# Ordering the last feed-forward, the shared expert and the expert copies of a four-stage sequence kernel

## The chip, the cores and the metric

The kernel runs on one core of a Trainium2 chip. The metric is the device time of one execution in microseconds. Each engine (PE is TensorE, DVE is VectorE, ACT is ScalarE, POOL is GpSimd, SP is SyncE, which issues most of the DMAs) works off its own instructions in a fixed order and waits for the others on semaphores. All orders are written out by hand.

## The reference

The input x has 4 sequences of 512 tokens, 128 wide. Four stages run one after the other, each added to x behind a layer norm:

```
x = x + recurrence(layernorm(x))        # h = h*A + x_t along the tokens, then h @ BC
x = x + local_layers(layernorm(x))      # 2 layers: local attention (8 heads, window 64), then
                                        #   h = norm(shift(y)); y = y + (a * gelu(g)) @ w2 + b2
x = x + attention(layernorm(x))         # 8 heads of 16 over the 512 tokens of a sequence
x = x + moe(layernorm(x))               # shared = (silu(x @ sg) * (x @ su)) @ sd
                                        # routed: expert argmax(x @ gate) of 32, rows scaled by
                                        #   sigmoid(max), silu(x @ g_e) * (x @ u_e) @ d_e
```

## The kernel before, in words

**Blocks.** The local layers run as 8 blocks of one sequence and one layer, each with 4 tiles of 128 tokens. Block 7 is the last sequence in the last layer. The generator `layer_steps()` yields the order of all steps, and every engine walks through the same list and issues its own part of each step. The steps of a block's feed-forward are `y_att` (DVE adds the product of the attention into y, L1062, and copies the unshifted half, L1066), `shift` (PE moves the other half by one token with two matmuls, L1534 and L1535, into bank 2 of PSUM; ACT copies it out, L783), `ff_stats`, `ff_rstd`, `ff_apply` (DVE L953, L957, L964, POOL L602), `hnT` (PE transposes, ACT scales, L1542 and L791), three times `up` (PE L1551, ACT gelu L797, DVE product L1072), `down` (PE L1560 in 24 matmuls, DVE L1081) and `base` (POOL).

**Drain and front.** After the loop over the 32 tiles, a tail of `layer_steps()` drains blocks 6 and 7. Steps of the global attention (`l1`) are woven into it: for sequence 1 the front is `apply` (DVE L964 into `y`), `pre` (PE transposes into bank 2, L1650, ACT L822), `qk` (PE L1656 and L1657, ACT) and `split` (ACT, POOL, and then the SP's stores). For sequence 0 there are six `max` steps (PE L1671 makes scores, DVE L1244 reduces them in 1.2 us each), and `sums`, two DVE reductions. `max` uses banks 4 and 5, `up` 20 and `qk` 1 banks 6 and 7. The following list, `l1_steps()`, starts with 16 more `max` steps, the last six of which need the query and key stacks of sequence 1. Work on the probabilities follows.

**Shared expert and slots.** The tail of `l1_steps()` holds the last sequence's norm and routing, and the shared expert of the four sequences. Its steps: `s_up b i` (PE, four matmuls, L1590), `silu` (ACT L803), `gate` (DVE product L1197), `s_down b` (PE, 16 matmuls, L1627, after both gates of b and after the `add` of b-2), `add b` (DVE adds to x, L1202; the semaphore `x4s` counts these). The steps `s_up`, `rank` and `row` take three pairs of banks in turn. For the routing: `route` (PE, then `choose` on DVE), `rank` (PE counts; 15 small DVE steps of `slots_b`, ending in L1182, give the slot of each row), `scale` (DVE multiplies the rows by their score, L1125), `scatter` (POOL, four indirect DMAs for each sequence, L691), `experts` and `row` (the list of experts, DVE L1297). The SP waits for all scatters, then loads the first rows (L571) and the row numbers (L573) and stores the four sequences of x as their `add` is done (L578).

**Routed experts.** 24 tiles of 4 x 32 rows, four experts each, run in a pipeline. Experts 1 to 3 of a tile have their weights copied from the resident `wx` to `w_copy`: two by DVE (`weights_one`, L1211), one by ACT (`weights_two`, L811). The expert's number is read from memory into a register (`value_load`, L1205 on DVE) before each copy. `copies 0` and `copies 1` are steps of the tail; the copies of tile 2 stand after it, behind a wait for the fourth `add`, since their places overlap the shared expert's products `act_s` in `region_b`. Then `gated(0)` and `gated(1)` (DVE L1358) follow, and the loop. POOL adds each tile's result to the output with an indirect DMA (L718), once the four stores have landed.

The change touches `places`, `l1_steps`, `layer_steps`, the ACT and the DVE code ahead of the routed loop.

Of the kernel before, what the change touches and what calls it, by code (L numbers as in the profile page):

```python
# [15 lines left out]
BATCH, SEQ = 4, 512  # L16
# [32 lines left out]
PER = 4  # L49
# [3 lines left out]
EW = 2 * INTER + IC * P  # L53
# [17 lines left out]
def build(nc, A, out):  # L71
    with ExitStack() as ctx:
# [10 lines left out]
        region_b = sb("region_b", [P, 10400])  # L83
# [147 lines left out]
        def copies(*places):  # L231
            return [region[:, at:at + EW] for region, at in places]

        places = copies(*((region_r, 2048 + n * EW) for n in range(PER)), (region_b, 0), (region_b, EW),
                        *((region_b, 4112 + n * EW) for n in range(2 * PER)), (region_r, 0))
        w_copy = [places[n * 3:n * 3 + 3] for n in range(WBUF)]
        xs_dram = nc.dram_tensor("xs_dram", (SLOT_ROWS, ROW), FP).ap()

# [33 lines left out]
        def l1_steps():  # L272

            n = BATCH * 16  # L280
            early = {7: (("val", 1),), 8: (("stat", 2),), 10: (("apply", 2),), 14: (("pre", 2),), 16: (("qk", 2),),
                     17: (("val", 2),), 18: (("split", 2),), 20: (("load", 2),)}
            late = {1: (("stat", 3),), 3: (("apply", 3),), 6: (("pre", 3),), 8: (("qk", 3),), 9: (("split", 3),), 13: (("load", 3),), 17: (("val", 3),),
                    43: (("rstat", 0), ("rstat", 1)), 44: (("rapply", 0),), 45: (("rapply", 1),), 47: (("rpre", 0),), 48: (("rpre", 1),),
                    50: (("rstat", 2),), 51: (("route", 0),), 52: (("rapply", 2),), 53: (("route", 1), ("scale", 0)),
                    55: (("rpre", 2), ("scale", 1)), 57: (("route", 2),), 59: (("scale", 2),), 60: (("rank", 0),),
                    61: (("scatter", 0),)}
            for m in range(DRAIN_MAX, LEAD):
                yield "max", m // 16, m % 16
                if m == 16:  # L290
                    yield "shift", 0, 0
                for what, b in early.get(m, ()):
                    yield what, b, 0
            for g in range(n):
                yield "probs", g // 16, g % 16
                m = g + LEAD
                if m < n:
                    yield "max", m // 16, m % 16
                if m % 16 == 0 and 16 < m <= n:
                    yield "shift", m // 16 - 1, 0  # L300
                if g % 16 == 1 and g > 16:
                    yield "end", g // 16 - 1, 0
                for what, b in late.get(g, ()):
                    yield what, b, 0

            last = BATCH - 1
            yield from (("s_up", 0, 0), ("end", last, 0), ("silu", 0, 0), ("rstat", last, 0), ("scatter", 1, 0), ("scatter", 2, 0),
                        ("gate", 0, 0), ("s_up", 0, 1), ("silu", 0, 1), ("gate", 0, 1), ("s_up", 1, 0), ("silu", 1, 0),
                        ("rapply", last, 0), ("s_up", 1, 1), ("gate", 1, 0), ("rpre", last, 0), ("silu", 1, 1), ("s_down", 0, 0),
                        ("gate", 1, 1), ("route", last, 0), ("add", 0, 0), ("s_up", 2, 0), ("silu", 2, 0), ("rank", 1, 0),  # L310
                        ("s_down", 1, 0), ("scale", last, 0), ("scatter", last, 0), ("gate", 2, 0), ("s_up", 2, 1), ("silu", 2, 1),
                        ("add", 1, 0), ("experts", 0, 0), ("gate", 2, 1), ("s_up", 3, 0), ("silu", 3, 0), ("s_down", 2, 0),
                        ("row", 0, 0), ("gate", 3, 0), ("s_up", 3, 1), ("silu", 3, 1), ("copies", 0, 0), ("gate", 3, 1),
                        ("add", 2, 0), ("copies", 1, 0), ("s_down", 3, 0), ("add", 3, 0))

        def up_banks(n):

# [9 lines left out]
        def layer_steps():  # L327
# [12 lines left out]
            def l1(*items, b=0, i=0):  # L340
                return [("l1", (what, b, i)) for what in items if what]
# [4 lines left out]
            for i in range(NTILES):  # L346
                t, k = i % NT, i // NT - 1
                up = {3: HC * k, 0: HC * (k - 1) + 1, 1: HC * (k - 1) + 2, 2: -1}[t]
                yield from of(NTILES, ("probs", i))
                yield from of(BLOCKS * HC, ("to_gelu", up))  # L350
                yield from of(NTILES, ("v", i + 3), ("ssq", i + 3))
                yield from early.get(i, ())
                if t == 0:
                    yield from of(BLOCKS, ("y_att", k))
                yield from l1({27: "stat", 28: "apply"}.get(i))
                if i == NTILES - 1:
                    yield from l1("stat", b=1)
                if t == 1:
                    yield from of(BLOCKS, ("ff_stats", k))
                yield from of(NTILES, ("vals", i), ("heads", i + 1), ("masks", i + 1))  # L360
                if t == 0:
                    yield from of(BLOCKS, ("shift", k))
                if t == 2:
                    yield from of(BLOCKS, ("hnT", k))
                if t == 3:
                    yield from of(BLOCKS, ("stream", k + 3))
                yield from fronts.get(i, ())
                yield from l1(*{28: ("pre",), 29: ("split", "load"), 30: ("wv",)}.get(i, ()))
                yield from of(NTILES, ("rotsum", i + 2))
                if t == 1:  # L370
                    yield from of(BLOCKS, ("ff_rstd", k))
                yield from of(NTILES, ("norm", i + 3))
                yield from of(BLOCKS * HC, ("up", up))
                if t == 2:
                    yield from of(BLOCKS, ("down", k - 1))
                if t == 3:
                    yield from of(BLOCKS, ("base", k))
                yield from of(NTILES, ("scores", i + 1))
                if i < NTILES - 1:
                    yield from of(BLOCKS * HC, ("to_exp", up))  # L380
                yield from of(NTILES, ("oT", i), ("qk", i + 4))
                if i == NTILES - 1:
                    yield "up", HC * k + 1
                    yield from l1("max")
                yield "wo", i
                if t == 1:
                    yield from of(BLOCKS, ("ff_apply", k))
                if i == 28:
                    yield from l1("qk")
                yield from of(NTILES, ("rot", i + 3))  # L390
            b, m = BLOCKS - 1, HC * BLOCKS
            yield from l1("zero")
            yield from l1("zero", b=1)
            yield from l1("apply", b=1)
            yield "y_att", b
            yield from l1("pre", b=1)
            yield "shift", b
            yield from l1("max", i=1)
            yield from (("ff_stats", b), ("ff_rstd", b), ("up", m - 4))
            yield from l1("qk", b=1)  # L400
            yield "ff_apply", b
            yield from l1("sums")
            yield "hnT", b
            yield from l1("split", b=1)
            yield "down", b - 1
            yield from l1("max", i=2)
# [318 lines left out]
        def _(a):  # L725
# [79 lines left out]
            def expert_two(j):  # L805
                return a.value_load(exp_of[0:1, PER * j + 3:PER * j + 4], min_val=0, max_val=EXP - 1)

            def weights_two(j, e):

                need(a, M["y_mm"], j - WBUF + 1)  # L810
                act_(w_copy[j % WBUF][2], wx[:, bass.ds(e, 1), :].rearrange("p a n -> p (a n)"), ACT.Copy)\  # L811
                    .then_inc(M["w_two"], 1)
# [105 lines left out]
            def back_sb(j):  # L918
                a.wait_ge(M["actT_mm"], j + 1)
                need(a, M["y_mm"], j - 1)  # L920
                act_(actT[j % 2], bank(4 + j % 2)[:, 0:INTER], ACT.Copy).then_inc(M["actT_sb"], 1)

            tokens_sb(0)
            tokens_sb(1)
            a.wait_ge(M["x4s"], BATCH)
            weights_two(2, expert_two(2))
            gate_sb(0)
            tokens_sb(2)
            e = expert_two(3)
            gate_sb(1)  # L930
            back_sb(0)
            for j in range(PAIRS):
                if j + 3 < PAIRS:
                    weights_two(j + 3, e)
                if j + 4 < PAIRS:
                    e = expert_two(j + 4)
                if j + 2 < PAIRS:
                    gate_sb(j + 2)
                if j + 3 < PAIRS:
                    tokens_sb(j + 3)  # L940
                if j + 1 < PAIRS:
                    back_sb(j + 1)
# [3 lines left out]
        def _(v):  # L946
# [419 lines left out]
                    v.wait_ge(ys_out[j % AHEAD], 16 * (j // AHEAD))  # L1366
                d.tensor_copy(ys[j % AHEAD], bank(6 + j % 2)[:, 0:P]).then_inc(M["y_sb"], 1)  # L1367

            weights_one(2, [expert_of(2, w) for w in (1, 2)])
            pair = [expert_of(3, w) for w in (1, 2)]  # L1370
            gated(0)
            gated(1)
# [555 lines left out]
```

## Time and profile before

| | |
|---|---|
| median of 3 runs | 682.47 us (680.77 to 684.91) |
| the profiled execution | 679.96 us, of it span of the instructions 678.1 us |
| busy | PE 87%, DVE 76%, ACT 53%, POOL 45% of the span |
| mean granted clock of TensorE | 0.958 |

An engine's busy share is a mean over very different stages. The start of the first feed-forward of block 7 lies at about 424 us, the last six `max` ahead of the probabilities at about 470 us, the shared expert from 586 us to 620 us, the routed loop from there to the end. A timeline row gives the start, the duration, the engine and line, what is written and read, and in brackets how long the engine was idle before it and what released it. A chain row gives start, duration, engine, output and line of one piece of the chain that ended last.

### The profile page before, as it was taken

The numbers are of one execution on the slowest core, as the hardware profiler recorded it, in microseconds if no ns is written. First come the engines' busy times: TensorE is split into PE (matmuls) and PEld (weight loads), VectorE is DVE, ScalarE is ACT, GpSimd is POOL, SyncE is SP. The second block draws the span as 40 slices with busy tenths as digits, with TensorE's granted clock in tenths as the row PEclk, the third lists the DMA queues.
The fourth block names the chain that finished last, engine by engine and source line by source line (L and its number), as shares of the span: only waits on it lengthen the run. The fifth ranks groups of instructions, "written<-read, shape, count | busy, mean of one in ns | idle before, by whom it ended". The sixth has DMA issues, their size and how long they took to land.

```text
span 678.1 us, 14399 instructions
## 1 busy us (share of the span) xinstructions
PE 587.9 (87%) x5382; PEld 343.5 (51%) x5382; DVE 517.0 (76%) x935; ACT 360.5 (53%) x566; POOL 306.5 (45%) x247
## 2 busy tenths in 40 slices
PE   3767678899999999999999888778899989987994
PEld 2244455666766767667667556432223324454442
DVE  6777888988889788888888754578877786574883
ACT  0223224477567575675774664312575667734872
POOL 2676444656354546464755633313120001251786
PEclk9768989999999999999999999896899999998998
DMA  8303000101010101010101035060966226214451
GB/s 262 85 17 117 17 17 17 26 17 25 18 33 9 34 17 26 18 25 17 34 9 34 17 82 122 19 127 4 217 202 189 95 94 212 71 32 106 60 66 11
DMA packets 33298, 44.03 MB, mean 65 GB/s; under 512 B 9249, under 2 KB 24653, under 8 KB 32461
## 3 DMA queue, kind: packets, MB, share of 16 engines
q1 hardware_dynamic: 29260, 40.99, 22.8%
q0 software_dynamic: 3968, 2.12, 2.4%
q8 instruction: 44, 0.72, 0.4%
q14 instruction: 26, 0.21, 0.1%
HBM read 27.54 MB, written 8.41 MB: 53 GB/s over the span
## 4 chain that ended last, share of the span: by engine, by line
PE 47%; DVE 29%; issue 11%; ACT 6%; POOL 4%; DVEq 1%; DMA 0%; POOLq 0%; ACTq 0%
PE ps L1551 5%; PE ps L1582 4%; DVE ssum L1012 4%; DVE smx L1042 3%; PE ps L1560 3%; PE ps L1687 3%; DVE mneg L1244 3%; PE ps L1773 3%; ACT region_r L853 2%; PE ps L1671 2%; DVE region_b L1020 2%; DVE region_r L1029 2%; DVE region_r L1037 2%; PE ps L1794 2%; PE ps L1504 2%
## 5 line engine op out<-in xcount | busy, mean ns | idle before, releaser
L624 POOL TENSOR_TENSOR rnorm<-ssum_c,neg_half 128x16 f32<-128x16 f32 x32 | 94.3, 2947 | 108.2 <-DVE ssum_c L1015 106.7
L636 POOL TENSOR_TENSOR region_r<-region_b,region_w 128x512 f32<-128x512 f32 x64 | 82.8, 1315 | 38.7 <-DVE region_b L1020 38.1
L1244 DVE TENSOR_REDUCE mneg<-ps 128x2 f32<-128x1024 f32 x64 | 77.1, 1219 | 22.2 <-PE ps L1671 21.2
L853 ACT ACTIVATE region_r<-ps 128x1024 f32<-128x1024 f32 x64 | 63.2, 1024 | 34.0 <-PE ps L1687 33.9
L746 ACT ACTIVATE region_w<-ps 128x1024 f32<-128x1024 f32 x32 | 32.8, 1025 | 64.2 <-PE ps L1438 64.2
L1437 PE MATMUL ps<-region_w,hT 128*128 128x512 f32 x64 | 37.6, 672 | 20.5 <-DVE region_b L1020 19.6
L600 POOL TENSOR_TENSOR var_eps<-mv,eps 128x4 f32<-128x4 f32 x20 | 8.0, 400 | 103.5 <-DVE mv L957 103.5
L731 ACT ACT_TABLE_LOAD x39 | 50.0, 1283 | 1.4 <-PEq L1920 0.7
L718 POOL DMA_INDIRECT out<-region_r x24 | 38.2, 1592 | 22.4 <-DVE region_r L1367 14.7
L1020 DVE TENSOR_TENSOR region_b<-ps,rnorm 128x1024 f32<-128x1024 f32 x32 | 39.1, 1221 | 11.8 <-POOL rnorm L624 10.9
L1551 PE MATMUL ps<-region_w 128*114 128x512 f32 x96 | 46.7, 610 | 0.6 <-ACT region_w L763 0.6
L1504 PEld LDWEIGHTS ps<-region_b,pts 128*64 128x64 f32 x512 | 32.2, 137 | 24.8 <-issue 24.8
L772 ACT ACTIVATE pts<-ps 128x512 f32<-128x512 f32 x64 | 34.9, 595 | 16.6 <-PE ps L1489 16.5
L1523 PEld LDWEIGHTS ps<-region_w,oT 128*128 128x128 f32 x256 | 34.0, 194 | 18.2 <-issue 11.4
L1012 DVE TENSOR_REDUCE ssum<-region_w 128x16 f32<-128x1024 f32 x32 | 38.7, 1211 | 4.9 <-ACT region_w L746 4.9
L1037 DVE TENSOR_TENSOR region_r<-region_r 128x1024 f32<-128x1024 f32 x32 | 41.4, 1294 | 0.3
L1042 DVE TENSOR_REDUCE smx<-ps 128x8 f32<-128x1024 f32 x32 | 38.9, 1215 | 2.3 <-PE ps L1479 2.3
L1045 DVE TENSOR_TENSOR region_b<-ps,smx 128x1024 f32<-128x1024 f32 x32 | 39.2, 1224 | 1.1
L1029 DVE TENSOR_TENSOR region_r<-region_b,region_w 128x1024 f32<-128x1024 f32 x32 | 39.7, 1240 | 0.0
L1504 PE MATMUL ps<-region_b,pts 128*64 128x65 f32 x512 | 36.6, 225 | 2.2 <-ACT pts L772 2.2
L778 ACT ACTIVATE oT<-ps 128x512 f32<-128x512 f32 x32 | 18.8, 586 | 35.2 <-PE ps L1512 35.2
L1523 PE MATMUL ps<-region_w,oT 128*128 128x128 f32 x256 | 34.4, 278 | 3.0 <-ACT oT L778 3.0
(277 smaller groups left out, 1419.0 us busy)
## 6 DMA issues: line engine op xcount, KB each, us to landing
region_w<-in_wx SPq DMA_DIRECT2D x16, 768.0 KB, 4.5
region_b<-region_w SPq DMA_DIRECT2D x56, 130.0 KB, 2.3
parts_dram<-region_b SPq DMA_DIRECT2D x6, 384.0 KB, 2.6
xs_dram<-region_w SPq DMA_DIRECT2D x1, 1548.0 KB, 7.3
region_w<-in_wqkv SPq DMA_DIRECT2D x2, 768.0 KB, 8.8
pts<-xs_dram SPq DMA_DIRECT2D x24, 64.0 KB, 2.0
region_w<-parts_dram SPq DMA_DIRECT2D x3, 384.0 KB, 6.8
region_b<-parts_dram SPq DMA_DIRECT2D x3, 384.0 KB, 7.3
```

What stands on the lines that cost most here:

```text
L624: g.tensor_tensor(rnorm[:, :], ssum_c[n % 2][:, :], neg_half[:, :], ALU.pow).then_inc(S["rnormed"], 1)
L636: g.tensor_tensor(dst, src, tab, ALU.mult).then_inc(S["rot_bb"], 1)
L853: act_(dst, bank(l1_bank[what, b, i], of=2), ACT.Exp).then_inc(T["ex"], 1)
L1012: d.tensor_reduce(ssum[:, :], sq.rearrange("p (h d) -> p h d", d=DH), AX.X, ALU.add).then_inc(S["ssq"], 1)
L1020: d.tensor_tensor(qn[n % 2].rearrange("p (h d) -> p h d", d=DH), bank(qk_bank(n), of=2).rearrange("p (h d) -> p h d", d=DH), rnorm[:, :].u ...
L1029: d.tensor_tensor(rot[n % 2].rearrange("p (z h d) -> p z h d", z=2, h=HEADS), qn[n % 2].rearrange("p (z h d) -> p z h d", z=2, h=HEADS), t ...
L1037: d.tensor_tensor(rot[n % 2], rot[n % 2], rotb[n % 2], ALU.add).then_inc(S["rotated"], 1)
L1042: d.tensor_reduce(smx[n % 2][:, :], sc, AX.X, ALU.max).then_inc(S["smax"], 1)
L1244: d.tensor_reduce(mneg[b % 2][:, 2 * i:2 * i + 2], bank(l1_bank[what, b, i], of=2) .rearrange("p (q t) -> p q t", q=2), AX.X, ALU.max, neg ...
L1504: last = mm(ps[w * WIN:(w + 1) * WIN, c0:c0 + VW], pts[n % 2][:, j, w * WIN:(w + 1) * WIN], vals[:, t, h, :], start=True, stop=True)
L1523: last = mm(bank(3)[:, t * P:(t + 1) * P], oT[n % 2][:, c, :], wo[k // BATCH][:, c, :], start=(c == 0), stop=(c == 3))
L1551: last = mm(ps[0:HW, n0 * BANK:(n0 + 1) * BANK], w1[k // BATCH][:, g, c, :], hnT, start=True, stop=True)
```

## The change

In the tail of `layer_steps()`, `y_att 7` moves ahead of `max 0` and of the front of sequence 1, `shift`, `ff_stats`, `ff_rstd` and `up 20`, `ff_apply` follow at once, and `apply`, `pre`, `qk` of sequence 1 and `max 1` come between or behind; `sums` moves behind `qk 1`. In the tail of `l1_steps()`, `scale 3` and the last scatter move ahead of or beside `rank 1`, the additions 0 and 1 move behind the slots, `row` ahead of the last `s_up`, `s_down 2` behind that, and a new step `copies 2` stands ahead of `add 3`. So that it can, the places of `w_copy[2]` become free of `act_s` (one of them lies in `rot_b` now), and the wait of ACT for `x4s` moves behind its first steps of the routed pipeline.

```diff
-                        *((region_b, 4112 + n * EW) for n in range(2 * PER)), (region_r, 0))
+                        (region_b, 4112), (rot_b, 0), (region_b, 4112 + 3 * EW),
+                        *((region_b, 4112 + n * EW) for n in (1, 2, 4, 5, 6, 7)))
...
-                        ("gate", 1, 1), ("route", last, 0), ("add", 0, 0), ("s_up", 2, 0), ("silu", 2, 0), ("rank", 1, 0),
-                        ("s_down", 1, 0), ("scale", last, 0), ("scatter", last, 0), ("gate", 2, 0), ("s_up", 2, 1), ("silu", 2, 1),
-                        ("add", 1, 0), ("experts", 0, 0), ("gate", 2, 1), ("s_up", 3, 0), ("silu", 3, 0), ("s_down", 2, 0),
-                        ("row", 0, 0), ("gate", 3, 0), ("s_up", 3, 1), ("silu", 3, 1), ("copies", 0, 0), ("gate", 3, 1),
-                        ("add", 2, 0), ("copies", 1, 0), ("s_down", 3, 0), ("add", 3, 0))
+                        ("gate", 1, 1), ("route", last, 0), ("s_up", 2, 0), ("silu", 2, 0), ("scale", last, 0), ("rank", 1, 0),
+                        ("scatter", last, 0), ("s_down", 1, 0), ("s_up", 2, 1), ("silu", 2, 1), ("gate", 2, 0), ("experts", 0, 0),
+                        ("s_up", 3, 0), ("silu", 3, 0), ("gate", 2, 1), ("add", 0, 0), ("add", 1, 0), ("row", 0, 0),
+                        ("s_up", 3, 1), ("silu", 3, 1), ("gate", 3, 0), ("s_down", 2, 0), ("copies", 0, 0), ("gate", 3, 1),
+                        ("s_down", 3, 0), ("copies", 1, 0), ("add", 2, 0), ("copies", 2, 0), ("add", 3, 0))
...
                 if i == NTILES - 1:
                     yield "up", HC * k + 1
-                    yield from l1("max")
                 yield "wo", i
...
             b, m = BLOCKS - 1, HC * BLOCKS
+            yield "y_att", b
+            yield from l1("max")
             yield from l1("zero")
+            yield "shift", b
             yield from l1("zero", b=1)
+            yield from (("ff_stats", b), ("ff_rstd", b))
             yield from l1("apply", b=1)
-            yield "y_att", b
+            yield from (("up", m - 4), ("ff_apply", b))
+            yield from l1("max", i=1)
             yield from l1("pre", b=1)
-            yield "shift", b
-            yield from l1("max", i=1)
-            yield from (("ff_stats", b), ("ff_rstd", b), ("up", m - 4))
+            yield "hnT", b
             yield from l1("qk", b=1)
-            yield "ff_apply", b
             yield from l1("sums")
-            yield "hnT", b
             yield from l1("split", b=1)
             yield "down", b - 1
...
-            a.wait_ge(M["x4s"], BATCH)
-            weights_two(2, expert_two(2))
             gate_sb(0)
...
             back_sb(0)
+            a.wait_ge(M["x4s"], BATCH)
...
-            weights_one(2, [expert_of(2, w) for w in (1, 2)])
             pair = [expert_of(3, w) for w in (1, 2)]
```

## Rows read from the trace of the kernel before

**Rows 1.** The page: busy times and the granted clock in 40 slices.
```profile
PE 587.9 (87%) x5382; PEld 343.5 (51%) x5382; DVE 517.0 (76%) x935; ACT 360.5 (53%) x566; POOL 306.5 (45%) x247
...
PEclk9768989999999999999999999896899999998998
```

**Rows 2.** Timelines by engine, drain of block 7: DVE, then PE, ACT, POOL.
```profile
422.25 1.22 DVE L1244 TENSOR_REDUCE mneg<-ps 128x2 f32<-128x1024 f32 x1
423.38 1.11 DVE L964 TENSOR_SCALAR y<-xr,mv,rstd 128x128 f32<-128x128 f32 x4
424.40 0.68 DVE L1062 TENSOR_TENSOR region_r<-region_r,ps 128x512 f32<-128x512 f32 x1
...
429.50 0.86 DVE L953 BATCH_NORM_STATS2 stats<-region_b 128x6 f32<-128x128 f32 x4
...
432.48 1.10 DVE L964 TENSOR_SCALAR region_b<-region_b,mv,rstd 128x128 f32<-128x128 f32 x4
...
437.93 0.69 DVE L1081 TENSOR_TENSOR xr<-region_r,ps 128x512 f32<-128x512 f32 x1 [2.09 <-PE ps L1560]
...
426.22 0.67 PE L1534 MATMUL ps<-region_r,down_one 128*128 128x256 f32 x2 [0.96 <-ACT region_r L822]
...
432.82 1.10 PE L1656 MATMUL ps<-region_r,region_w 128*128 128x512 f32 x2 [1.77 <-DVE region_b L1072]
...
435.05 2.84 PE L1560 MATMUL ps<-region_w,region_b 114*128 114x128 f32 x24
...
427.51 0.38 ACT L783 ACTIVATE region_b<-ps 128x256 f32<-128x256 f32 x1 [1.44 <-PE ps L1535]
...
431.14 1.02 POOL L602 TENSOR_TENSOR rstd<-var_eps,neg_half 128x4 f32<-128x4 f32 x1
```

**Rows 3.** The chain that ended last, in the same stretch.
```profile
428.32 2.74 PE ps L1551 x4
...
442.81 1.72 PE ps L1551 x4
```

**Rows 4.** Stretches of 2 us: busy times, granted clock, DMA share, GB/s.
```profile
428.00:430.00 2.00, 2.00 (x4) 0.81 (x4) 1.64 (x4) 0.00 (x0) 0.00 (x0) 0.50 0.00 0
...
460.00:462.00 2.00, 0.88 (x3) 0.13 (x2) 2.00 (x4) 0.00 (x0) 0.00 (x0) 0.50 0.00 0
...
618.00:620.00 2.00, 2.00 (x10) 1.65 (x9) 0.66 (x2) 0.13 (x1) 0.00 (x0) 0.50 0.99 46
```

**Rows 5.** Timelines by engine, from the slots to the last addition: DVE, then PE, SP.
```profile
607.13 0.17 DVE L1182 CAST region_r<-region_r 128x4 uint32<-128x4 f32 x1
...
607.69 0.69 DVE L1125 TENSOR_TENSOR region_b<-region_b,region_r 128x512 f32<-128x512 f32 x1
...
613.14 0.25 DVE L1297 TENSOR_SCALAR region_r<-ps 1x96 int32<-1x96 f32 x1 [2.40 <-PE ps L1644]
...
615.16 1.03 DVE L1211 COPY region_r<-region_w 128x768 f32 x2 [1.19 <-issue]
...
619.66 0.69 DVE L1202 TENSOR_TENSOR xr<-xr,ps 128x512 f32<-128x512 f32 x1 [1.34 <-PE ps L1627]
...
609.03 1.98 PE L1590 MATMUL ps<-region_b,region_r 128*128 128x512 f32 x4 [1.87 <-DVE region_b L1197]
...
616.84 2.78 PE L1627 MATMUL ps<-region_r,region_b 128*128 128x128 f32 x16 [1.83 <-DVE region_b L1197]
...
615.25 1.75 SPq L571 DMA_DIRECT2D pts<-xs_dram  x4
```

**Rows 6.** Timelines: DVE ahead of the routed loop, POOL's first and last output.
```profile
622.68 1.03 DVE L1211 COPY region_b<-region_w 128x768 f32 x2 [2.33 <-issue]
624.36 0.75 DVE L1358 TENSOR_TENSOR region_r<-region_r,ps 128x256 f32<-128x256 f32 x2 [0.65 <-ACT region_r L916]
...
628.62 1.61 POOL L718 DMA_INDIRECT out<-region_r  x1 [14.71 <-DVE region_r L1367]
...
672.95 1.55 POOL L718 DMA_INDIRECT out<-region_r  x1 [0.30 <-issue]
```

## The prediction

> **What bounds the kernel now.** I read the page first. PE is busy 87% of the span and DVE 76% [rows 1], so neither is the bound throughout, and the granted clock has dips below 9 around slices 26 to 29 and near the end. The views that decide are the timelines of the two places that the edits touch, with the chain of waits laid over them.
>
> In the drain of block 7 the chain changes hands from step to step. DVE is free for the last attention product at 422.25, but reduces `max 0` (1.22) and applies the front of sequence 1 (1.11) before `y_att` starts at 424.40. The shift matmuls start at 426.22, 1.1 after the 425.1 at which y was ready: they share bank 2 with `pre 1`, and the bracket names ACT, which reads that. The shifted half is out at 427.9, but the statistics start at 429.50, behind `max 1`. The `up` in the middle of this runs 2.74 [rows 3] with the clock at 0.50 [rows 4], where another takes 1.72 [rows 3]. `ff_apply` starts at 432.48. Then PE does `qk 1` from 432.82, transposes, and starts `down 6` at 435.05, whose sum goes out at 437.93 [rows 2].
>
> At the other end the reader is to see three waits of PE or DVE, each for something that the order put late: PE idles 1.87 until `gate 2 0` (behind the slots and `scale`), 1.83 until the last gate (behind the list of experts and its first copies), and DVE needs 1.19 and 2.33 for register loads [rows 5, 6]. From `gated(0)` at 624.36 on, the loop is a fixed train: the first output leaves POOL at 628.62 and the last at 672.95 [rows 6], 44.33 for 23 steps, 1.93 each.
>
> **The change, drain of block 7.** No arithmetic instruction is added or removed; what counts is when the last links come. New times, from the old durations:
> - `y_att` starts at 422.25 instead of 424.40 (its product is there: PE no longer does `max 0` first). It takes 0.68, the copy about 0.25: y at 422.95.
> - The shift matmuls start at about 423.0, since bank 2 is not yet used by `pre 1`. By the old start and end they take 1.3, ACT 0.38: out at 424.75. DVE fills the time with `max 0`, 423.2 to 424.4, which therefore costs nothing.
> - The statistics run 424.8 to 426.1 (0.86 and the aggregation; from their start at 429.50 to POOL's start at 431.14, less POOL's first small step, it was 1.3). POOL's power takes 1.02 and ends at 427.4. DVE covers this wait with the application for sequence 1 (1.1), to 427.2.
> - PE: `up 20` behind the shift, 424.3 to 426.0 at full clock (1.72), gelu and `gated` (together 1.4, from the old `up`'s end at 431.06 to 432.48); `gated`, half of that, waits for DVE, free at 427.2, and ends at 427.85. `ff_apply` 427.85 to 428.9, against 432.48 before. This is 4.6 earlier.
> - PE: `hnT` 429.0 to 429.6, `qk 1` to 431.35, `down 6` at 431.4 against 435.05: 3.7 earlier. A part of the 4.6 is given back, because `hnT` now stands ahead of `qk 1` and is late for it, while `qk 1` alone could start at 428.6.
> - `sums`, `split`, POOL's parts and the SP's stores follow `qk 1` and come 3 to 3.6 earlier. The `load` behind them is wanted only by `max` steps far back in the following list. `max 1` stands ahead of `sums`, in DVE's slack before `down 6`.
>
> From `down 6` on the order is the old one, so it is carried along: the sum out at 434.2 for 437.93. **Drain: 3.7.** Bounds: 2.15, if only the two DVE steps ahead of `y_att` are saved; 4.6, the advance of `ff_apply`. What follows until the shared expert waits only on things that themselves move (stacks, first weights, statistics), so I let the 3.7 pass undiminished.
>
> **The shared expert.** The time of the slots themselves, 607.30, stays: they wait for PE's ranks. But `scale` (607.2 to 608.38 in the old order) moves into DVE's wait ahead of them, where the addition of sequence 0 and a gap stood, so that:
> - `gate 2 0` is 1.0 earlier, and with it PE's next `s_up`: 608.0 for 609.03. The last scatter of POOL waits for the slots alone and is 1.1 earlier too; the SP's first row loads start at 614.15 for 615.25, land some 2 later, ahead of the use I find below (617).
> - `row` follows that `s_up` at once (609.9) and not `s_down 2` as well: the list of experts at 610.6 instead of 613.14, 2.5 earlier. The two additions stand ahead of it on DVE, in the time that PE needs for the `s_up`.
> - DVE: `gate 3 0` 611.3, loads of two registers (1.19 of visible gap) and `copies 0` (1.03) to 613.5, `gate 3 1` 613.5 to 614.1. PE has done the last `s_up` and `s_down 2` until 613.95, so the gap of 1.83 ahead of `s_down 3` goes: start at 614.15 for 616.84, 2.7 earlier.
> - `s_down 3` took 2.78, with the clock at 0.50 [rows 4]; by the ratio of the two `up`s, 2.74 to 1.72, it would be 1.75 at full clock. It ends at about 616. But DVE now has `copies 1` (1.03), `add 2` (0.69), and `copies 2` (1.03, with 0.3 of loads not hidden) ahead of `add 3`: this one starts at 617.2 and ends at 617.9, for 620.35. **2.4 earlier**, and here the copies take back 1.2 of what PE gives.
> - Behind `add 3` DVE had loads 2.33, copies 1.03, loads 0.65: 4.0 to `gated(0)`. Now only one pair of loads, taken at 2.33: `gated(0)` at 620.2 for 624.36. ACT's side is ready before (rows at 616.5, transposed, matmul, silu by about 619).
>
> **Shared expert and start of the loop: 4.2.** Bounds: 2.4, the advance of `add 3` alone (the moved copies only traded), and 5.3, if the pair of loads costs the 1.19 of the other visible gap. I take the 2.33, since these loads stand behind the same kind of wait. The new places of the copies have the same size, and I give the loop its old step; none of its instructions changes. The stores of the output are the other condition of POOL's start: the DMA engines are filled by the row numbers and the stores (share 0.99, 46 GB/s [rows 4]), all of which start 1.1 to 2.5 earlier, so that they are done at about 623.2, ahead of POOL's 624.4. That is a margin of 1.
>
> **Sum.** 3.7 and 4.2 are 7.9. The profiled execution takes 679.96 with a span of 678.1; it would take 672.1. The median of the three runs is 2.5 above that execution, so 682.47 - 7.9 = 674.6, which is 1.2% less.
>
> **The clock, a rule against it.** The clock stood at 0.50 at 428, 460 and 618 [rows 4], each time after a stretch with little matmul work. By the rows alone, both short dips lose their cause: PE gets `up 20` directly behind the shift, and work without the two gaps of 1.8 at the end.
> The Trainium skill (TensorE: Matmul & The Clock Gate, Part 1) has the activity window of this gate run freely, so that a fall can come at another place in an execution of the same code. By that rule, the new idle spots, small as they are, can be hit: this is the first rival, and the sum would be about 2 less for each hit.
>
> **Rivals.**
> - *The clock falls in the new order.* PE has about 2 of idle time in 426.5 to 429, and again ahead of `gated(0)` (618.5 to 620.7). A fall makes `qk 1` and `down 6` run at half rate, or the first two tiles of the loop, 1.7 to 2.0 each if it lasts as the one at 428 did (about two such 2 us stretches at half speed). One: 676.5. Both: 678.4. For: three dips in the old trace. Against: PE idled longer before these. 0.20.
> - *The drain's gain is absorbed* in the stretch of `max` steps behind it, for instance by a DMA of the stacks that does not move with it. Only 4.2 stay: 678.3. Against: the chain there is DVE's own work. 0.07.
> - *The last steps do not come earlier*: POOL's start is set by the stores and the row numbers, DVE's additions wait for the copies. Then the end gives 0 to 1 and the clock eats part of the drain: about 681. 0.06.
> - *Slower.* The long dip (clock 0.50 at 460 with DVE at 2.00 of 2.00 [rows 4]) costs little because PE waits for DVE's reductions there. If, shifted, it outlasts them and reaches the first probabilities, where PE is the bound, each us of half clock there loses up to 0.5. It decides from some 16 us of dip more, 7.9 lost; at 20 more the time is 684.6. Nothing in the profile speaks for so long a one. 0.05.
>
> **How the numbers follow.** Forecast as worked out 0.62, with an own range of 672 to 677 from the bounds of the two parts (4.6 to 9.9, ends thinned). The range 671.8 to 679.7 takes in the clock rival and the absorbed drain, and leaves out about 0.15. A measurement of this kernel tells a change from none from about 0.5%, or 3.4 us, on: faster is below 679.1. Faster: 0.62, nearly all of 0.20, and half of 0.07, 0.83 in all. Same: the rest of these and the 0.06, 0.12. Slower: 0.05.
>
> **What would show it.** In the trace after: `y_att` of block 7 directly behind the last `gated`, its shift without a wait for ACT, an `up` of 1.7 and not 2.7 behind it, `down 6` at about 431.4. With the drain's 3.7 taken off: L1297 near 606.9, the last `s_up` and `s_down` without gaps, the last L1202 ending near 614.2, the first `gated` near 616.5, the first L718 near 620.7, and 1.93 between outputs. It is wrong if the `max` stretch begins earlier but the probabilities do not, if the loads behind `add 3` cost over 3, or if the loop's step changes.

## The result, and the profile after

The changed kernel takes 676.33 us (median of 8 runs, 672.03 to 679.85); the kernel before, run beside it, took 683.44 (8 runs, 680.77 to 684.91). The ratio is 0.9892, 95% interval 0.9865 to 0.9919. The medians are 7.1 us apart. The forecast was 674.6, faster.

The profiled execution takes 676.56 with a span of 674.8, only 3.4 below the one before (679.96 and 678.1). The page, with the clock in 40 slices:

```profile
PE 587.7 (87%) x5382; PEld 343.2 (51%) x5382; DVE 517.4 (77%) x935; ACT 360.8 (53%) x566; POOL 307.2 (46%) x247
...
PEclk9778999999999999999999999996799999999997
```

The sums are those of [rows 1] within 0.7 us; no work was added. The dip that stood in slice 26 before is gone. Another fall of the clock, from 384.7 to 388.1, is too short to show as a digit in its slice; it lies ahead of everything that was changed. The section on why the prediction was right works out what both did to the 3.4.

First, two rows of the kernel before: the `gated` product from which the drain is counted and the `up` at half clock:

```profile
421.58 0.75 DVE L1072 SCALAR_TENSOR_TENSOR region_b<-ps,b,region_w 114x512 f32<-114x512 f32 x1 [1.41 <-ACT region_w L797]
...
428.12 2.94 PE L1551 MATMUL ps<-region_w 128*114 128x512 f32 x4
```

The drain of block 7, timelines of DVE and then PE in the kernel after, for [rows 2, 3]. The columns are start, duration, engine, line, operation, and in brackets the idle time before it with what ended it.

```profile
423.63 0.75 DVE L1072 SCALAR_TENSOR_TENSOR region_b<-ps,b,region_w 114x512 f32<-114x512 f32 x1 [1.40 <-ACT region_w L798]
424.30 0.68 DVE L1062 TENSOR_TENSOR region_r<-region_r,ps 128x512 f32<-128x512 f32 x1
...
426.56 0.87 DVE L953 BATCH_NORM_STATS2 stats<-region_b 128x6 f32<-128x128 f32 x4
...
429.43 1.11 DVE L964 TENSOR_SCALAR region_b<-region_b,mv,rstd 128x128 f32<-128x128 f32 x4
...
435.68 0.69 DVE L1081 TENSOR_TENSOR xr<-region_r,ps 128x512 f32<-128x512 f32 x1 [1.76 <-PE ps L1559]
...
425.03 0.70 PE L1533 MATMUL ps<-region_r,down_one 128*128 128x256 f32 x2 [0.83 <-DVE region_r L1062]
425.89 1.88 PE L1550 MATMUL ps<-region_w 128*114 128x512 f32 x4
...
432.80 2.84 PE L1559 MATMUL ps<-region_w,region_b 114*128 114x128 f32 x24
```

`y_att` (L1062) begins 0.67 after the start of the last `gated` product, the shift's bracket now names the addition and not ACT, and the `up` behind it runs 1.88 where it ran 2.94 (2.74 as a piece of the chain [rows 3]): it no longer meets a half clock.

The other end, DVE, PE, SP and POOL after, for [rows 5, 6]:

```profile
605.04 0.17 DVE L1182 CAST region_r<-region_r 128x4 uint32<-128x4 f32 x1
608.14 0.25 DVE L1297 TENSOR_SCALAR region_r<-ps 1x96 int32<-1x96 f32 x1
614.64 0.68 DVE L1202 TENSOR_TENSOR xr<-xr,ps 128x512 f32<-128x512 f32 x1
616.65 0.42 DVE L1358 TENSOR_TENSOR region_r<-region_r,ps 128x256 f32<-128x256 f32 x1 [1.32 <-ACT region_r L917]
...
623.21 0.33 PE L1761 MATMUL ps<-ident,pts 128*128 128x128 f32 x1 [2.51 <-DMA pts<-xs_dram]
...
612.46 1.75 SPq L572 DMA_DIRECT2D pts<-xs_dram  x4
614.73 3.65 SPq L579 DMA_DIRECT2D out<-xr  x4
...
623.86 1.83 POOL L719 DMA_INDIRECT out<-region_r  x1 [12.94 <-DMA out<-xr]
628.95 1.69 POOL L719 DMA_INDIRECT out<-region_r  x1 [1.37 <-DVE region_r L1367]
669.64 1.55 POOL L719 DMA_INDIRECT out<-region_r  x1 [0.30 <-issue]
```

And two stretches of 2 us there (busy PE, weight loads, DVE, ACT, POOL; then clock, DMA share, GB/s):

```profile
618.00:620.00 2.00, 2.00 (x31) 0.89 (x27) 1.50 (x4) 2.00 (x6) 0.00 (x0) 1.00 0.97 284
...
624.00:626.00 2.00, 2.00 (x24) 0.69 (x16) 1.15 (x3) 0.92 (x2) 1.70 (x2) 0.50 0.12 33
```

Counted from the start of the span, the first product of the loop (L1358) is 7.7 earlier, but the first output only 4.8, and its bracket names a DMA: the stores of `xr`. PE waits 2.51 for the rows of a later tile, behind them in SP's queue, and then the clock falls.

### The profile page after: what moved, and what is told of

It is laid out like the page before. It is cut to its first block, busy times and chain, and to the rows that moved or that the text cites. A ratio compares the mean times of both kernels' runs of the same rounds, so it can differ in the third digit from the quotient of the medians.

```text
span 674.8 us, 14399 instructions
## 1 busy us (share of the span) xinstructions
PE 587.7 (87%) x5382; PEld 343.2 (51%) x5382; DVE 517.4 (77%) x935; ACT 360.8 (53%) x566; POOL 307.2 (46%) x247
## 4 chain that ended last, share of the span: by engine, by line
PE 47%; DVE 28%; issue 12%; ACT 6%; POOL 4%; DMA 2%; POOLq 0%; DVEq 0%; SPq 0%; ACTq 0%
PE ps L1550 5%; PE ps L1581 4%; DVE ssum L1012 4%; DVE smx L1042 3%; PE ps L1686 3%; PE ps L1559 3%; PE ps L1772 3%; DVE mneg L1244 3%; ACT region_r L854 2%; DVE region_b L1020 2%; PE ps L1670 2%; DVE region_r L1029 2%; DVE region_r L1037 2%; PE ps L1793 2%; DVE region_r L1055 2%
## 5 line engine op out<-in xcount | busy, mean ns | idle before, releaser
L779 ACT ACTIVATE oT<-ps 128x512 f32<-128x512 f32 x32 | 18.8, 586 | 36.2 <-PE ps L1511 36.2
L1478 PEld LDWEIGHTS ps<-region_w 64*64 64x64 f32 x1024 | 28.5, 135 | 17.8 <-issue 15.8
```

## The experiments

The code below shows each edit against the kernel after, with "..." where lines are left out.

All times below that begin with a plus are counted from the start of the same instruction in each trace: in the drain from the last `gated` product (L1072) ahead of `y_att` of block 7 (421.58 before, 423.63 after), at the end from the start of L1182 [rows 5], the slots.

### Each half of the change alone

`drain_only` is the change with only the hunk in `layer_steps()`; the rest is as in the kernel before:

```diff
-                        ("s_down", 3, 0), ("copies", 1, 0), ("add", 2, 0), ("copies", 2, 0), ("add", 3, 0))
...
+                        ("add", 2, 0), ("copies", 1, 0), ("s_down", 3, 0), ("add", 3, 0))
...
+            weights_one(2, [expert_of(2, w) for w in (1, 2)])
```

> The kernel before with the new order of the drain of block 7 alone. Theory: the last sum of block 7 goes out 4.3 us earlier, counted from the start of the last gated product ahead of y_att (25.35 us behind it in the kernel after, 29.65 us in the one before), and nearly all of it (4.1) reaches the end, since the stages behind move with it: ratio to before 0.994. Rival (the gain is absorbed in the max stretch): ratio 1.000. Rival (the whole gain of the change is here): 0.989.

`tail_only` has only the others, with the old drain:

```diff
+                    yield from l1("max")
...
-            yield "y_att", b
-            yield from l1("max")
...
-            yield "shift", b
...
+            yield "y_att", b
+            yield from l1("pre", b=1)
+            yield "shift", b
```

> The kernel before with the new tail alone (order of the shared expert, places of the copies, copies of tile 2 ahead of the last addition). Theory: gated(0) starts 5.6 us earlier against the end of the slots (12.3 us behind L1182 started, at 11.6 in the kernel after and 17.2 in the one before), but the DMA engines, filled with the row numbers and the four stores, hold the rows of tile 4 and the stores back, so that only 1 to 3 us reach the end: ratio 0.996 to 0.998. Rival (the step passes on its 5.6 us): 0.992. Rival (it gives nothing): 1.000.

Measured: `drain_only` 678.31, ratio 0.9953 (0.9926 to 0.9981), by which it gains 3.2 us; `tail_only` 679.14, ratio 0.9960 (0.9931 to 0.9989), 2.7 us. The medians alone lie 4.2 and 3.4 below the 682.50 of the kernel before, run beside them. The product of the two ratios is 0.9913, within the interval of the whole change. Both halves work, and neither needs the other.

| | before | after | drain_only | tail_only |
|---|---|---|---|---|
| sum of block 6, from L1072 | +16.35 | +12.05 | +12.05 | +16.36 |
| sum of block 7, from L1072 | +29.65 | +25.35 | +25.35 | +29.66 |
| from there to the reciprocal that ends the probabilities (L1263) | 140.17 | 140.34 | 140.34 | 140.19 |
| list of experts, from the slots | +6.01 | +3.10 | +6.01 | +3.10 |
| last addition | +12.53 | +9.60 | +11.81 | +9.61 |
| first `gated` of the loop | +17.23 | +11.61 | +16.73 | +11.62 |
| first output | +21.49 | +18.82 | +21.77 | +17.03 |
| last output | +65.82 | +64.60 | +66.92 | +62.24 |

DVE's sum of block 6 in `drain_only`:

```profile
423.78 0.75 DVE L1072 SCALAR_TENSOR_TENSOR region_b<-ps,b,region_w 114x512 f32<-114x512 f32 x1 [1.40 <-ACT region_w L797]
...
435.83 0.69 DVE L1081 TENSOR_TENSOR xr<-region_r,ps 128x512 f32<-128x512 f32 x1 [1.76 <-PE ps L1560]
```

That is 12.05, for 16.35 between 421.58 and 437.93 [rows 2]. And the ends of `tail_only`, DVE, POOL and PE:

```profile
607.35 0.17 DVE L1182 CAST region_r<-region_r 128x4 uint32<-128x4 f32 x1
...
624.38 1.61 POOL L719 DMA_INDIRECT out<-region_r  x1 [11.15 <-DMA out<-xr]
669.59 1.55 POOL L719 DMA_INDIRECT out<-region_r  x1 [0.30 <-issue]
...
624.74 0.33 PE L1761 MATMUL ps<-ident,pts 128*128 128x128 f32 x1 [1.79 <-DMA pts<-xs_dram]
```

Its list, addition and first `gated` stand within 0.02 of the kernel after, with waits for the same DMAs, but without the fall of the clock in the loop's first tiles. The four stores are issued at the same distance from the slots in both (+9.69 and +9.50); the slowest of them takes 5.3 us to land in the kernel after and 3.7 here. This part of the code is the same, so the 1.8 between the first outputs is a matter of single executions and not of the order.

### The stores ahead of the row loads

The stores of the first two sequences wait for nothing but their additions. Here they go out ahead of the wait for the scatters, in the kernel after (`early_stores`) and in the one before (`before_early_stores`):

```diff
+            x_store(0)
+            x_store(1)
             sp.wait_ge(M["scattered"], 16 * TILES)
...
-            for b in range(BATCH):
-                sp.wait_ge(M["x4s"], b + 1)
...
+            x_store(2)
+            x_store(3)
```

> The kernel after, with the stores of sequences 0 and 1 issued by the SP ahead of its wait for the scatters instead of behind the row loads. Theory (the DMA engines are what eats the tail's gain): the wait of PE's fifth transpose of rows for its DMA (2.5 us in the profile after) shrinks to under 1, POOL's first output no longer waits for the stores, the clock does not fall at 624 us, and the time drops by 2 to 4 us: ratio to before about 0.985. Rival (POOL's train of outputs or PE's loop sets the end anyway): as the kernel after, 0.989. Rival (the early stores delay the scatters): slower than after.

> The kernel before with the same two stores ahead of the wait for the scatters. Theory: in the old order the loop starts late (gated(0) at 624.4 us, when the DMA engines are nearly done, at 624.5), so the stores hide and moving them gives under 0.7 us: ratio 0.999 to 1.001. Rival (the stores cost in any order): 0.996 or less.

Measured: `early_stores` 675.42, ratio 0.9891 (0.9861 to 0.9922); `before_early_stores` 681.17, ratio 0.9994 (0.9973 to 1.0015). In the profile of the first the waits for the DMAs are gone. SP, then POOL of `early_stores`:

```profile
610.52 0.99 SPq L573 DMA_DIRECT2D out<-xr  x2
...
624.70 1.61 POOL L724 DMA_INDIRECT out<-region_r  x1 [11.07 <-DVE region_r L1372]
...
669.02 1.55 POOL L724 DMA_INDIRECT out<-region_r  x1 [0.30 <-issue]
```

POOL waits for its own rows again, at +16.73, and the last output is at +61.05, 1.2 earlier than in `tail_only` (neither has a fall of the clock there). From the first `gated` to the last output it takes 48.8, as in the kernel before (48.6), where `tail_only` takes 50.6. So in the traces the stores cost the new order 1.2 to 1.8. The times don't tell it: 0.9891 and 0.9892 are the same, and the 2 to 4 us that I expected did not come. In the old order moving them gives nothing, as expected: there the stores had their cover.

The same pair again on another chip, where the kernel before takes 694.62:

> The kernel after, once more, on the chip of the runs beside it. The two profiles of the new drain so far both have a dip of the clock at 384.7 us, ahead of every changed instruction, which costs 1.7 us; the three of the old drain have none there. Theory (the place of a dip is chance): ratio 0.989 again, and in this profile the dip at 385 us may be gone; the last sum of block 7 stays 25.3 us behind the last gated product ahead of y_att. Rival (the new order itself brings the dip): it is there again.

> The kernel with the early stores once more, beside the kernel after. Theory: the wait of POOL and PE for the DMA engines is gone in each execution, so it is 1.2 to 2.5 us faster than the kernel after of the same call (from the start of the last step of the slots to the last output 61.0 us against 62.2 without and 64.6 with a dip of the clock). Rival: no difference between the two medians beyond 0.5 us.

Measured: `after_again` 686.86, ratio 0.9902 (0.9868 to 0.9936); `early_stores_b` 684.69, ratio 0.9878 (0.9850 to 0.9906). Again no difference outside the intervals; the 1.2 to 2.5 us expected are not shown. In the profiles the last output is at +67.31 and +67.47. This pair can't price the stores: in `early_stores_b` the clock stood at half until 611.2, past the slots, so that its list of experts is 1.15 and its first output 0.8 later than in `after_again`. The train from first to last output takes 50.05 in `after_again`, 2.18 for each of 23 steps, and 49.41 in `early_stores_b`, against 1.93 a step on the first chip [rows 6]. PE's waits in the loop of `after_again` have "issue" as their releaser; why this chip's loop is slower I did not settle.

### The copies 2 back behind the last addition

```diff
-                        ("s_down", 3, 0), ("copies", 1, 0), ("add", 2, 0), ("copies", 2, 0), ("add", 3, 0))
+                        ("s_down", 3, 0), ("copies", 1, 0), ("add", 2, 0), ("add", 3, 0))
...
+            a.wait_ge(M["x4s"], BATCH)
+            weights_two(2, expert_two(2))
...
-            a.wait_ge(M["x4s"], BATCH)
...
+            weights_one(2, [expert_of(2, w) for w in (1, 2)])
```

> The kernel after, but the copies of tile 2 stand behind the last addition again. Theory: the last addition ends 1.2 us earlier (without the 1.0 of copies ahead of it), but gated(0) comes 2 us later than in the kernel after (loads 2.3 or 1.1, copies 1.0, loads 0.65 behind the addition). Since the stores and the rows then bound POOL's first output in the kernel after, the time is within 1 us of it: ratio 0.989 to 0.991. Rival (the copies were the tail's gain, as the forecast had it with 1.7 of 4.2 us): 0.992.

Measured: 686.54, ratio 0.9898 (0.9870 to 0.9927), that of the whole change on the same chip (0.9902). The last addition is at +8.96, 0.65 earlier than in `after_again`, the first `gated` at +12.66, 0.9 later, and the first output at +17.23 for +17.26: equal. The move of the copies does what it should to the first product, and nothing comes of it: in `after_again` the first output waits for the stores, here for its own rows, and both come at the same time.

This profile has a fall of the clock in the new drain, from 433.6 to 437.0, under `qk 1` and `down 6`, where the prediction's first rival put it. DVE, then PE:

```profile
425.72 0.75 DVE L1073 SCALAR_TENSOR_TENSOR region_b<-ps,b,region_w 114x512 f32<-114x512 f32 x1 [1.40 <-ACT region_w L798]
...
439.44 0.69 DVE L1082 TENSOR_TENSOR xr<-region_r,ps 128x512 f32<-128x512 f32 x1 [3.44 <-PE ps L1561]
...
434.42 1.92 PE L1658 MATMUL ps<-region_r,region_w 128*128 128x512 f32 x2
```

The sum of block 6 is at +13.72 here for +12.05: the fall costs this drain 1.67.

### `y_att` ahead, the rest of the drain in the old order

```diff
             yield "y_att", b
             yield from l1("max")
             yield from l1("zero")
-            yield "shift", b
             yield from l1("zero", b=1)
-            yield from (("ff_stats", b), ("ff_rstd", b))
             yield from l1("apply", b=1)
-            yield from (("up", m - 4), ("ff_apply", b))
...
+            yield from l1("pre", b=1)
+            yield "shift", b
+            yield from l1("max", i=1)
+            yield from (("ff_stats", b), ("ff_rstd", b), ("up", m - 4))
+            yield from l1("qk", b=1)
+            yield "ff_apply", b
```

> The kernel after with the drain in its old order, except that y_att and max 0 stand first. Theory (the shift must also leave bank 2 before pre 1): the shift now waits for apply, pre and ACT behind max 0, so the last sum of block 7 comes 29 to 30.5 us behind the last gated product ahead of y_att (old 29.65, after 25.35): no gain from y_att alone, ratio as that of the tail alone, 0.996. Rival (each step that is earlier passes on its share, 2.15 us): 27.5 us, ratio 0.992.

Measured: 690.83, ratio 0.9961 (0.9943 to 0.9979), what the tail alone gives (0.9960). DVE, PE, DVE of `yatt_only`:

```profile
421.39 0.68 DVE L1062 TENSOR_TENSOR region_r<-region_r,ps 128x512 f32<-128x512 f32 x1
...
426.29 1.19 PE L1533 MATMUL ps<-region_r,down_one 128*128 128x256 f32 x2 [0.96 <-ACT region_r L823]
...
437.80 0.69 DVE L1081 TENSOR_TENSOR xr<-region_r,ps 128x512 f32<-128x512 f32 x1 [1.52 <-PE ps L1559]
```

The addition is early, but the shift stands in PE's list behind `pre 1` and waits for ACT to empty bank 2, as in [rows 2]. It starts at +5.56, even 0.92 later than before (+4.64), because `y_att` now stands ahead of `apply`, for which `pre 1` waits. The sum of block 6 is at +17.07, 0.72 later than before. The clock falls at 425.9 (the shift runs 1.19 for 0.70), but that is no difference to the kernel before: there it falls at the same distance from the `gated` product (+5.18 here, +5.24 there) and for as long. So the drain's gain lies in the shift ahead of `pre 1` and what follows it, not in `y_att`. Which of the steps behind the shift gives how much was not taken apart.

### Small matmuls in the `max` stretch

In this stretch, between the drain and the probabilities, the kernels before and after alike have a mean clock of some 0.7, which is half clock for 16 to 17 of 28 us. PE waits for DVE's reductions there, so I gave it something to do: with the stores early, eight small bf16 products of the identity into a free bank behind each of the sixteen `max` steps ahead of the probabilities. Their results go nowhere.

```diff
                     last.then_inc(T["d_mm"], 1)
+                    if DRAIN_MAX <= 16 * b + i < LEAD:
+                        claim((7,))
+                        for _ in range(8):
+                            mm(bank(7)[:, 0:P], ident_b[:, :], ident_b[:, :], start=True, stop=True)
```

> The kernel with the early stores, and behind each of the 16 max steps ahead of the probabilities and beside the first of them eight small bf16 matmuls (128 x 128) of constants into bank 7, which nobody reads before it is overwritten. They keep PE busy in the stretch where the clock was at half speed for 10 to 13.7 us in every profile, old and new. Theory: the dip at 454 to 457 us goes, the two pairs of front matmuls (1.8 each at half clock) take 0.9 each, DVE's gap of 1.7 to 2.7 behind them closes, and the span from the last sum of block 7 to the last sequence's end of attention, 140.3 us, falls by 1.5 to 3 us; time 2 us below the early stores. Rival (DVE's reductions set this stretch at any clock of PE): under 0.5 us. Rival (the extra matmuls delay the max steps): slower.

> The kernel with the early stores, a third time, beside the kernel after and the one with the small matmuls. Theory: 1 to 2 us below the kernel after of this call. Rival: within 0.5 us, since on a chip where PE waits for its own instructions in the loop the train of outputs is set by them.

> The kernel after, a third time. Theory: ratio 0.989 to 0.990; the last sum of block 7 25.35 us behind the last gated product ahead of y_att; if there is no dip at 385 us, y_att of block 7 is 43.0 us behind that of block 6, and 44.7 us if there is one (45.2 in the old order without a dip).

Measured, on the second chip (before 694.46): `filler` 682.35, ratio 0.9839 (0.9805 to 0.9873); `early_stores_c` 687.11, 0.9890 (0.9851 to 0.9929); `after_c` 686.26, 0.9896 (0.9862 to 0.9930). The stretch in `after_c`:

```profile
452.00:480.00 28.00, 21.97 (x66) 6.63 (x66) 24.37 (x43) 7.84 (x12) 7.44 (x12) 0.70 0.28 61
```

and in `filler`:

```profile
452.00:480.00 28.00, 23.71 (x174) 11.64 (x171) 27.18 (x44) 11.67 (x15) 7.77 (x12) 1.00 0.39 83
```

One product of a front in this stretch, PE of the kernel after and then of `filler`:

```profile
464.30 2.00 PE L1655 MATMUL ps<-hT,region_w 128*128 128x512 f32 x2
```

```profile
461.34 1.10 PE L1660 MATMUL ps<-hT,region_w 128*128 128x512 f32 x2
```

108 more matmuls stand in the same 28 us, PE's busy time grows by 1.7 only, since each other matmul is shorter, and DVE is busy 27.2 of 28 instead of 24.4: it had waited for PE at half clock. From the sum of block 7 to the last reciprocal it is 139.27 for 142.36, 3.1 less, and the whole of that is there at the first of the four reciprocals (57.56 for 60.66). The clock is held in the other executions too: the mean granted clock of whole runs is 0.968 over six runs of `filler`, 0.956 and 0.952 in `early_stores_c` and `after_c`. This version has lower medians than both kernels: `filler` against `early_stores_c` differs by those matmuls alone, and is 4.8 lower in the median, 3.9 lower than `after_c`. The intervals to the kernel before overlap by a little (0.9851 to 0.9873); the 3.1 of the trace, in the very stretch that was changed, bears the medians out. `early_stores_c` is 0.9 above `after_c` in the median, not the 1 to 2 below that I expected of it.

## Why the prediction was right

**Drain.** The 3.7 was 4.30, near the upper bound of 4.6, within 0.01 in each of the eight profiles with the new order and no fall of the clock in it. By steps: `y_att` at once (+0.67, as forecast), `ff_apply` at +5.80 for +6.27, `down 6` at +9.17 for +9.82. The shift took 1.06 to ACT's start, where I had 1.3, and the statistics were out a little sooner. The chain after it, `qk 1` ahead of `down 6` included, went as worked out.

Not all of the 4.30 is the order's. All four profiles with the old order behind `y_att` (before, `tail_only`, `before_early_stores`, `yatt_only`) have a fall of the clock in this drain, at 425.9 to 428.8; of the nine with the new order only `no_copies2` has one, and its sum of block 6 is at +13.72. With a fall of the same length on both sides, though not under the same steps, the order is worth 2.63, and the fall that is missing 1.67 (`no_copies2` ran on the second chip, where the new order without a fall gives the same +12.05 as on the first). The prediction's 3.7 held both without saying so: it took `up` at the 1.72 of full clock. That the new order loses the fall bears out what the prediction said of the drain, that the dip there loses its cause; but four of the nine (the kernel after among them) have one at 385 to 388 instead, ahead of the changed code, and none of the four with the old order. Over whole runs the mean granted clock hardly moves, 0.955 over the 29 runs of the kernel before that stand beside it and 0.957 over the 12 of `drain_only`. So how much of the 1.67 reaches the median is open; the ratio of `drain_only` gives 3.2, with 1.3 to 5.1 in its interval.

**Absorbed?** No. Sum of block 7 and last reciprocal, before and then after:

```profile
451.23 0.69 DVE L1081 TENSOR_TENSOR xr<-region_r,ps 128x512 f32<-128x512 f32 x1 [1.91 <-PE ps L1560]
...
591.40 0.36 DVE L1263 RECIPROCAL arec<-ps 128x32 f32<-128x32 f32 x1 [4.02 <-PE ps L1716]
```

```profile
448.98 0.69 DVE L1081 TENSOR_TENSOR xr<-region_r,ps 128x512 f32<-128x512 f32 x1 [1.91 <-PE ps L1559]
...
589.32 0.36 DVE L1263 RECIPROCAL arec<-ps 128x32 f32<-128x32 f32 x1 [4.02 <-PE ps L1715]
```

From the sum of block 7 to the reciprocal the kernel takes 140.17 before and 140.34 after: 0.17 of 4.30 is lost in 140 us. `drain_only` shows the same 140.34.

**The clock.** The rival had it fall at one of the new idle spots. In the profile after it did, at 623.6, behind PE's 2.51 wait, and it fell at a place that no edit touched. PE after, then PE before, `up` in block 6:

```profile
385.01 3.41 PE L1550 MATMUL ps<-region_w 128*114 128x512 f32 x4
```

```profile
384.50 1.88 PE L1551 MATMUL ps<-region_w 128*114 128x512 f32 x4
```

The instructions up to there are the same in both kernels. From `y_att` of block 6 to the last `gated` product ahead of that of block 7 it takes 44.04 after and 42.35 before, 1.7 more. `after_c` and `after_again`, the same program, have no fall there.
The Trainium skill (TensorE: Matmul & The Clock Gate, Part 1) says that the activity window of this gate runs freely, so that at a kernel's start the point of the transition changes from run to run. The three profiles of this one program show that the place of a fall in its middle changes as well: the first one behind 340 us comes at 384.7, 454.4 and 454.8.

So the profiled spans add up as follows: +0.36 ahead of block 6's `y_att`, +1.7 for this fall, −4.30 in the drain, +0.17 to the reciprocal, −1.22 from the slots to the last output, −3.3 in all. The kernel before had its own fall at 618 [rows 4], so the one at 623.6 stands against that. It also had one in the drain, from 426.8 to 430.2, and the one at 384.7 stands against it: in these two profiles the +1.7 gives back what the missing fall had brought to the 4.30. The profiled 3.3 is thus the difference of two executions with equally many short falls. The rest to 7.1 lies within the spread of single executions, 4 to 8 us for each kernel; the profiled execution of the kernel before, at 679.96, is below all eight of those beside the kernel after.

The rival's mechanism is real, then, and hit the profiled execution at the loop, and that of `no_copies2` in the drain for 1.67, where the rival had 1.7 to 2.0. The median does not show it. The slower rival, a long dip that reaches the probabilities, did not happen: the stretch after the drain kept its length.

**The shared expert.** List of experts 2.91 earlier (2.5 forecast), last addition 2.93 (2.4). The first `gated` came 5.62 earlier where I had 4.2, beyond the bound of 5.3. Behind `add 3` there is 1.33 in all, with ACT as the releaser, where I had 2.33 for the register loads. The last steps do come earlier; that rival falls too.

**The step that failed** is the stores: "done at about 623.2, ahead of POOL's 624.4. That is a margin of 1." Counted like the table, the stores were to be done at +16.1 and the first output to go at +17.3. But the loop starts 1.4 sooner than I had it (`gated` at +11.61 for +13.0), and the stores, issued behind the row loads and row numbers, are done at +17.0 in `tail_only` and at +18.8 in the kernel after. The first output waited for them in both, and PE waited 1.8 to 2.5 for the rows of a later tile behind them. That +17.03 lies near the +17.3 is luck: the loop was ready earlier and the stores later than worked out. The term of 4.2 measured 1.22 where both profiles have a fall of the clock at the loop's start (before and after), 2.41 where neither has one (`before_early_stores` +64.65, `tail_only` +62.24), 3.58 from the fall before to none in `tail_only`, and 2.7 by the ratio of `tail_only` (3.4 between the medians). So the forecast total of 7.9 came near the 7.1 in part by luck: in the traces the drain gave 0.6 more and the tail 0.6 to 3.0 less.

**Left open:** whether the stores' 1.2 to 1.8 in the traces is worth anything in the median. Early against late stores gave 0.9891 and 0.9892, 0.9878 and 0.9902, 0.9890 and 0.9896: none of the three tells it apart.

## What to carry to other kernels

In a fixed order, look for the step that waits for a buffer that a step of something else has just filled: the shift and its followers behind `pre 1` cost 2.6 us at like clock and 4.3 with the fall of the clock that stood there, and the operation at their head, moved alone, gave nothing. When a move makes compute earlier, check each of the other conditions of the next output for the same advance; a margin of 1 us in a sum of this length is none. Compare steps from a common instruction on, because two executions can differ by 1.7 us in code that no edit touches, and look in both for the falls of the clock between the two points.

## What the runs showed of the hardware

A stretch of 28 us in which PE waits for DVE ran at a mean granted clock of 0.70 (`after_c`); with 108 small matmuls in its waits it ran at 1.00 throughout, and the whole kernel got 0.5% to 0.7% faster. Work without a use, on an engine that isn't the bound, paid because the bound's next operand comes from it.

A fall of the clock comes at the same or another place from one execution of a program to the next (in the three profiles of the kernel after: at 384.7, 456.4, 473.4 and 623.6; at 454.4, 471.5 and 604.6; at 454.8, 475.3 and 605.0), and one cost 1.7 where PE sets the pace (at 384.7; and in `no_copies2`, with one at 433.6, the sum of block 6 is at +13.72 for +12.05).

The same program is 1.6% slower on the second chip (694.5 for 683.4). In the routed loop of the kernel after a step takes 2.18 there (`after_again`), where `early_stores` and the kernel before take 1.93 on the first. From the last reciprocal to the slots it takes 19.7 to 19.9 us in all seven profiles of that chip, 15.7 in all six of the first; the clock falls there, at 600 to 611, in the seven and in none of the six, and in `after_again` the matmuls of `s_down 1` stand apart there with "issue" as their releaser. The cause is open. Ratios to the kernel before were alike on both: 0.9892 against 0.9902 and 0.9896.
